# Keys and values of the second attention projected behind the routing of each group and kept in DRAM

## The reference

```
x = x + attention0(layernorm(x), ctx)          # 16 heads of 8, with biases
x = x + experts0(layernorm(x))                 # 32 experts of width 96, 4 for each token
x = x + attention1(layernorm(x), ctx, mask)    # 16 heads of 64, no biases
x = x + experts1(layernorm(x))                 # 8 experts of width 64, 2 for each token, and a shared one
# attention1
Q = (queries @ Wq) * mask;  K = (ctx @ Wk) * mask;  V = (ctx @ Wv) * mask
attn = softmax(Q K^T / 8) * mask;  attn = attn / sum(attn);  out = (attn V) @ Wo
```

## Time and profile before

| | us |
|---|---|
| median of 3 runs | 1396.31 (1390.09 to 1398.15) |
| profiled execution | 1396.49 |
| its span | 1394.7 |
| first attention | 0 to 311.5 |
| routing | 311.5 to 523.5 |
| tiles of experts | 523.5 to 663 |
| second attention, lead-in | 663 to 738 |
| second attention, steps | 738 to 1200 |
| last FFN | to 1394.7 |

### The profile page before, as it was taken

How to read it: one execution, slowest core, us unless ns; L and a number is a source line. 1 busy time by engine, 2 the same in 40 slices (tenths; PEclk the granted TensorE clock), 3 DMA queues, 4 the chain that set the end, 5 groups by cost and what they waited for, 6 DMA issues and landing times. The chain is left out here.

```text
span 1394.7 us, 27126 instructions
## 1 busy us (share of the span) xinstructions
PE 943.3 (68%) x10014; PEld 749.4 (54%) x10014; DVE 756.2 (54%) x1922; ACT 569.0 (41%) x901; POOL 604.3 (43%) x566
## 2 busy tenths in 40 slices
PE   1488778771101008998056999999999998471998
PEld 1356566540000007998024776777777778371886
DVE  3455655424554334554265676676767654267565
ACT  1166666642211104666034545544444443121554
POOL 1266775655778752444654424324241000020454
PEclk9878987755555558999579999999999999555999
DMA  4211111009111146775110000000000000100001
GB/s 131 80 58 48 55 59 53 23 8 245 40 46 42 49 144 171 202 203 159 40 40 24 20 17 24 17 18 23 17 21 6 1 2 2 34 5 0 9 23 30
DMA packets 100541, 76.33 MB, mean 55 GB/s; under 512 B 13045, under 2 KB 91810, under 8 KB 100418
## 3 DMA queue, kind: packets, MB, share of 16 engines
q1 hardware_dynamic: 61506, 43.04, 11.0%
q0 software_dynamic: 8192, 16.79, 3.9%
q10 hardware_dynamic: 30720, 14.82, 3.6%
HBM read 42.78 MB, written 31.59 MB: 53 GB/s over the span
## 5 line engine op out<-in xcount | busy, mean ns | idle before, releaser
L833 POOL DMA_INDIRECT fetched_a<-rows_y,chosen_row x128 | 122.5, 957 | 214.5 <-DVE x_all L707 178.1
L438 POOL TENSOR_TENSOR p_lo_a<-probs_a,p_hi_a 128x1024 f16<-128x1024 f32 x64 | 136.3, 2130 | 88.7 <-ACT p_hi_a L297 88.6
L588 PE MATMUL psum<-v_x_a,probs_a 128*128 128x65 f32 x1024 | 140.3, 280 | 29.8 <-DVE att_a L768 28.4
L1268 POOL DMA_INDIRECT rows_x<-rows_r,index_r x128 | 135.4, 1058 | 54.0 <-issue 39.2
L588 PEld LDWEIGHTS psum<-v_x_a,probs_a 128*128 128x128 f32 x1024 | 125.5, 193 | 46.1 <-DVE att_a L768 37.1
L752 DVE TENSOR_REDUCE negmax_a<-psum 128x8 f32<-128x1024 f32 x64 | 78.2, 1221 | 48.9 <-PE psum L571 42.9
L1423 POOL TENSOR_TENSOR h_lo_t<-hidden_t,h_hi_t 96x512 f16<-96x512 f32 x48 | 55.3, 1153 | 90.7 <-ACT h_hi_t L1395 90.7
L354 DVE TENSOR_REDUCE negmax_a<-psum 128x8 f32<-128x1024 f32 x64 | 78.3, 1223 | 26.1 <-PE psum L168 26.0
L1769 POOL TENSOR_TENSOR w_lo_f<-weighted_f,w_hi_f 128x512 fp32r<-128x512 f32 x40 | 51.9, 1297 | 93.0 <-ACT w_hi_f L1711 93.0
L296 ACT ACTIVATE probs_a<-psum 128x1024 f32<-128x1024 f32 x64 | 65.5, 1023 | 50.0 <-PE psum L152 49.8
L1054 PE MATMUL psum<-ident_x,rows_r 128*128 128x128 f16 x64 | 8.3, 310 | 114.1 <-DVE rows_r L1151 98.0
(11 more groups left out here) (336 smaller groups left out, 3137.8 us busy)
## 6 DMA issues: line engine op xcount, KB each, us to landing
listed_t<-rows_x SPq DMA_DIRECT2D x96, 128.0 KB, 2.4
rows_y<-result_t ACTq DMA_DIRECT2D x48, 256.0 KB, 2.3
q_pad_a<-narrow_q SPq DMA_DIRECT2D x64, 64.0 KB
k_x_a<-narrow_k SPq DMA_DIRECT2D x24, 128.0 KB
rows_x<-zeros_r SPq DMA_DIRECT2D x17, 128.0 KB
narrow_q<-q_hl_a SPq DMA_DIRECT2D x8, 256.0 KB, 2.0
narrow_k<-k_hl_a SPq DMA_DIRECT2D x8, 256.0 KB, 2.0
rows_x<-rows_r,index_r POOLq DMA_INDIRECT x128
```

The lines of the kernel that those rows point to most:

```text
L438: nc.gpsimd.tensor_tensor(p_lo[:, s % RING0, :], probs[:, s % NPR, :], p_hi[:, s % RING0, :], ALU.subtract).then_inc(s_plo, 1)
L588: last_ = nc.tensor.matmul(o, probs[:, s % 3, q], v_x[:, par, b % GB, h, :], start=True, stop=True)
L833: nc.gpsimd.indirect_dma_start(fetched[:, b % 2, k, :], None, rows_y, bass.IndirectOffsetOnAxis(ap=chosen["row"][:, b, k:k + 1], axis=0)). ...
L1268: nc.gpsimd.indirect_dma_start(rows_x, bass.IndirectOffsetOnAxis(ap=index[:, g * GB + t, k:k + 1], axis=0), rows[:, g % 2, t, :, :].rearra ...
```

## The change

For each group, keys and values of `attention1` are made in the routing stage. The context is masked in place by ScalarE; `keep` makes one context item, eight value items and eight key items in one run over three PSUM banks, behind ranks(g) and logits(g + 1) on TensorE, behind the scores of g + 1 on ScalarE; on VectorE their lower parts (`lower`) stand behind choose(g) and the rows of g + 1, ahead of choose(g + 1). SyncE stores them in DRAM, 2.1 MB of keys and 2.1 MB of values a group. In `attention1` SyncE loads them into the buffers that the items filled before, two groups at once and each later one when its buffer is free. The items c, k and v leave `work1`, with GpSimd's context and column. The weights are loaded and split in another order (wv and wk ahead of the first scores, w2 late, its raw copy in the place of w1's), ranks and logits share PSUM banks, and some pairs of semaphores are merged.

The core of the diff:

```diff
-    table = {0: (1, "k0 k1", ""), 1: (1, "q2 k2", "q3 k3"), 2: (1, "q4 k4", ""), 3: (1, "q5 k5", "q6 k6"),
-             4: (1, "q7 k7", ""), 5: (1, "v0 v1", "v2 v3"), 6: (1, "v4 v5", ""), 7: (1, "v6 v7", "")}
+    heads = {0: "q1", 1: "q2", 2: "q3", 3: "q4", 4: "q6", 5: "q7"}
     group = s // 8 + 1
-    head += fills(group, table[rel][1])
-    tail += fills(group, table[rel][2])
+    head += fills(group, heads.get(rel, ""))
+    if rel == 3:
+        tail += fills(group, "q5")
     if rel == 6:
         tail += fills(s // 8 + 2, "x")
     if rel == 7:
-        tail += fills(s // 8 + 2, "c q0 q1")
+        tail += fills(s // 8 + 2, "q0")
...
+        @block.sync
+        def _(sp):
+            for g in range(G):
+                if g >= 2:
+                    sp.wait_ge(s_sc, 8 * (g - 2) + 8)
+                for n in range(2):
+                    for part, k_half in enumerate((k_a, k_b)):
+                        sp.dma_start(k_half[:, g % 2, 4 * n:4 * n + 4, :], keys[g, n, :, part]).then_inc(s_keys[g % 2], 16)
+                if g >= 2:
+                    sp.wait_ge(s_pv, 2 * (8 * (g - 2) + 8))
+                for n in range(2):
+                    sp.dma_start(v_x[:, g % 2, 2 * n:2 * n + 2, :, :], vals[g, n]).then_inc(s_vals[g % 2], 16)
...
-                    await_free(("k", (b // GB, 4 * j + 3)))
+                    pe.wait_ge(s_keys[par], 64 * (b // GB // 2 + 1))
+                    await_free(("q", (b // GB, 4 * j + 3)))
...
-                        pe.wait_ge(s_vcol, s // 8 + 1)
-                        await_free(("v", (s // 8, 7)))
+                        pe.wait_ge(s_vals[par], 32 * (s // 16 + 1))
...
+        LG, RK = ([psum[:, n, 0:GB * E0], psum[:, n, 256:256 + GB * E0]] for n in (2, 3))
+        CNT, ROW = psum[:, 4, 0:128], psum[:, 4, 128:512]
+        KV = [psum[:, 5 + n, :] for n in range(3)]
...
+        parts = [(raw_later[0][:, :], w_v[0][:, :], w_v[1][:, :]), (raw_later[1][:, :], w_k[0][:, :], w_k[1][:, :]),
+                 (raw_later[2][:, :], later["wq"][0][:, :], later["wq"][1][:, :]),
+                 (raw1, record[:, :, W1_HI], record[:, :, W1_LO]),
                  (raw3[:, :, :], record[:, :, W3_HI], record[:, :, W3_LO]),
-                 (raw2[:, :, :], record[0:I0, :, W2_HI], record[0:I0, :, W2_LO])]
-        raw_later = [rt(f"raw_later{n}", [P, H * D1]) for n in range(3)]
-        parts += [(raw_later[n][:, :], later[name][0][:, :], later[name][1][:, :]) for n, name in enumerate(("wq", "wk", "wv"))]
-        raw_sel = rt("raw_sel", [P, 8, P])
+                 (raw2, record[0:I0, :, W2_HI], record[0:I0, :, W2_LO])]
+        c_hi, c_lo = rt("c_hi", [P, 512], F16), rt("c_lo", [P, 512], F16)
+        k_out, v_out = rt("k_out", [P, 2, 2, 4, 512], F16), rt("v_out", [P, 2, 2, H, D1 + 1])
+        s_masked, s_kv, s_kv_hi, s_kv_lo, s_v = (rsem(n) for n in ("masked", "kv", "kv_hi", "kv_lo", "v"))
+        s_k_out, s_v_out, s_parted = [rsem(f"k_out{n}") for n in range(2)], [rsem(f"v_out{n}") for n in range(2)], rsem("parted")
+        made = [("c", 0)] + [("v", n) for n in range(8)] + [("k", n) for n in range(8)]
+        FINE = 9
...
+                def store_values(g, n):
+                    sp.wait_ge(s_v, 8 * g + 4 * n + 4)
+                    sp.dma_start(vals[g, n], v_out[:, n, :, :, :]).then_inc(s_v_out[n], 16)
+
+                def store_keys(g, n):
+                    sp.wait_ge(s_kv_lo, FINE * g + 1 + 4 * n + 4)
+                    sp.dma_start(keys[g, n], k_out[:, n, :, :, :]).then_inc(s_k_out[n], 16)
...
+                for g in range(G):
+                    for n in range(2):
+                        store_values(g, n)
+                    for n in range(2):
+                        store_keys(g, n)
+                    if g == 3:
+                        sp.wait_ge(s_parted, 4)
+                        sp.dma_start(raw2, a["L0_ffn_w2"].rearrange("e i h -> i e h")).then_inc(s_raw[5], 16)
+                        sp.dma_start(raw_sel, a["c_sel1"]).then_inc(s_late, 16)
+                        sp.dma_start(later["wo"][:, :, :],
+                                     a["L1_xattn_Wo"].rearrange("(c p) h -> p c h", p=P)).then_inc(s_late, 16)
...
+                def keep(g, first, last):
+                    for at in range(first, last):
+                        kind, n = made[at]
+                        o = KV[(len(made) * g + at) % 3]
+                        if len(made) * g + at >= 3:
+                            older, before = divmod(len(made) * g + at - 3, len(made))
+                            if made[before][0] == "v":
+                                pe.wait_ge(s_v, 8 * older + made[before][1] + 1)
+                            else:
+                                pe.wait_ge(s_kv_lo, FINE * older + (0 if before == 0 else 1 + made[before][1]) + 1)
+                        if kind == "c":
+                            pe.wait_ge(s_masked, g + 1)
+                            for t in range(GB):
+                                last_ = nc.tensor.transpose(o[:, t * P:(t + 1) * P],
+                                                            ctx_all[:, (g * GB + t) * D:(g * GB + t + 1) * D], ident[:])
+                        elif kind == "v":
+                            if n == 0:
+                                pe.wait_ge(s_kv_lo, FINE * g + 1)
+                            if g == 0 and n == 0:
+                                pe.wait_ge(s_parted, 1)
+                            t, half_ = divmod(n, 2)
+                            cols, tok = slice(half_ * 512, half_ * 512 + 512), slice(t * P, (t + 1) * P)
+                            nc.tensor.matmul(o, c_hi[:, tok], w_v[0][:, cols], start=True, stop=False)
+                            nc.tensor.matmul(o, c_hi[:, tok], w_v[1][:, cols], start=False, stop=False)
+                            last_ = nc.tensor.matmul(o, c_lo[:, tok], w_v[0][:, cols], start=False, stop=True)
+                        else:
+                            if g == 0 and n == 0:
+                                pe.wait_ge(s_parted, 2)
+                            cols = slice(n * P, (n + 1) * P)
+                            nc.tensor.matmul(o, w_k[0][:, cols], c_hi[:, :], start=True, stop=False)
+                            nc.tensor.matmul(o, w_k[0][:, cols], c_lo[:, :], start=False, stop=False)
+                            last_ = nc.tensor.matmul(o, w_k[1][:, cols], c_hi[:, :], start=False, stop=True)
+                        last_.then_inc(s_kv, 1)
...
+                logits(0)
+                for g in range(G):
+                    ranks(g)
+                    if g + 1 < G:
+                        logits(g + 1)
+                    keep(g, 0, 17)
...
+                def masked(g):
+                    for t in range(GB):
+                        b = g * GB + t
+                        c = ctx_all[:, b * D:(b + 1) * D]
+                        last_ = nc.scalar.activation(c, c, ACT.Copy, scale=const["mask"][:, b:b + 1])
+                    last_.then_inc(s_masked, 1)
...
+                def keep(g, first, last):
+                    for at in range(first, last):
+                        kind, n = made[at]
+                        o = KV[(len(made) * g + at) % 3]
+                        act.wait_ge(s_kv, len(made) * g + at + 1)
+                        if kind == "c":
+                            nc.scalar.activation(c_hi[:, :], o, ACT.Copy).then_inc(s_kv_hi, 1)
+                        elif kind == "v":
+                            t, half_ = divmod(n, 2)
+                            b = g * GB + t
+                            if g and n % 4 == 0:
+                                act.wait_ge(s_v_out[n // 4], 16 * g)
+                            if half_ == 0:
+                                nc.scalar.activation(v_out[:, t // 2, t % 2, :, D1], const["unit"][:, :], ACT.Copy,
+                                                     scale=const["mask"][:, b:b + 1])
+                            nc.scalar.activation(v_out[:, t // 2, t % 2, half_ * 8:half_ * 8 + 8, 0:D1],
+                                                 o.rearrange("p (h d) -> p h d", d=D1), ACT.Copy,
+                                                 scale=const["mask"][:, b:b + 1]).then_inc(s_v, 1)
+                        else:
+                            if g and n % 4 == 0:
+                                act.wait_ge(s_k_out[n // 4], 16 * g)
+                            nc.scalar.activation(k_out[:, n // 4, 0, n % 4, :], o, ACT.Copy).then_inc(s_kv_hi, 1)
...
+                upper_rows(0)
+                split(0, parts[0])
+                split(1, parts[1])
+                grades(0)
+                for g in range(G):
+                    if g + 1 < G:
+                        upper_rows(g + 1)
+                        grades(g + 1)
+                    keep(g, 0, 17)
+                    if g + 1 < G:
+                        masked(g + 1)
+                    if g in (0, 1, 2):
+                        split(g + 2, parts[g + 2])
```

(42 more changed lines are left out.)

178 lines of the change are left out of this document (70 added, 108 removed).

## The result

| | median, us | of before |
|---|---|---|
| before | 1393.2 (1381.65 to 1398.15, 4 runs) | |
| after | 1492.78 (1487.09 to 1493.95, 4 runs) | 1.0715 (1.0657 to 1.0772) |

Slower, as forecast, but by 99.6 us (96.5 against the median shown ahead) where 43 were forecast. The profiled span is 1489.9 us, 95.2 more than before.

What follows compares the result with a forecast made beforehand. VectorE's in-order chain was to bound routing, as TensorE paces the second attention. Routing +104, attention running -57 and lead-in -4 gave +43 on 1396.5: 1440 us, with 1400 to 1500 for 8 in 10.

Steps and rivals of the forecast that it cites:

- terms 1 to 3: Routing: the run in VectorE's order makes groups 32.2 us, plus weight splits and last group: +91.7 us, 3 off for pads.
- term 4: Routing: VectorE's unexplained waits for ranks, 22.5 us in before, now count whole on its chain: +15 us (0 to 45).
- The third rival: Traffic stalls the supply: stores and loads lengthen unexplained waits in routing, lead-in and attention; 1498 us, chance 0.11.
- the low clock: Routing: TensorE's clock stays low, so each run takes 25.5 us, eight of them +55; 1495 us, chance 0.12.
- The likeliest: The case of VectorE's chain as worked out, bounding routing: 1440 us, own range 1405 to 1480, chance 0.67.
- The rule weighed: Instruction refills share DMA engines with queues, so 33.8 MB of stores would lengthen each refill, moving the sum nearer the third rival.
- term 5: Second attention, running: period falls to 50.3 us, gaining 8.3 in six groups and 7.3 in the last: -57 (-42 to -76).
- term 6: Second attention's lead-in: sixteen of 24 items go, against 8.5 MB of loads at the start: -4 us (-12 to +10).
- Cover holds: Rival: GpSimd's scatter, 24 us a group, stays routing's bound and the run is free; about 1348 us, chance 0.10.
- the clock never rises: Rival in routing: TensorE rests between runs, so its clock stays low and a run takes 25.5 us; 1495 us, chance 0.12.

Runs made afterwards that it cites:

- C: Chip of a later round; the changed kernel re-run there unedited: 1395.7 us, 1.0226 of before, which took 1365.11 us there.
- A: Chip of the main result, its number not recorded; changed kernel 1492.78 us against before's 1393.2 us, 1.0715.
- D: Chip of a later round; the changed kernel re-run there unedited: 1486.25 us, 1.0763 of before, which took 1379.85 us there.
- no_stores_again: Changed kernel with the routing stage's stores of keys and values left out for groups 1 to 7, on D: 1479.49 us, 1.0714 of before.
- B: Chip of the first follow-ups; before took 1367.45 us there; changed kernel with 26 dummy matmuls a group added: 1390.53 us, 1.0153 of before.
- E: Chip of a later round; the changed kernel re-run there unedited: 1392.43 us, 1.019 of before, which took 1366.16 us there.
- keys_first: Changed kernel with keys made before values and the next group's ranks amid the values on TensorE, on B: 1360.17 us, 0.995 of before.
- keys_first_2: keys_first with VectorE's weight subtraction and ScalarE's cast moved into waits: 1339.95 us, 0.982 of before on C; 1423.09 us, 1.0305 on D.

## Why the prediction was right and wrong

*The chain (terms 1 to 3) was right, and a little too long.* On C, from first scatter to pad rows, it is 241.5 us, forecast 256.0 without stalls. A clean group is 30.7 where 32.2 were forecast: the context 2.1 us (2.6), eight values 7.6 (8.1), the keys with their end 7.2 (7.5). The splits add 9 us up to the last group where 12.3 were set, and the tail after it is 17.9 (18.3). TensorE ran four items at a pitch of 0.43 and then at 0.21, as put. The stage's end was cheaper than forecast: 20.0 us from the pad rows on in place of 32.8, a gain of 12.8 for which 3 were set. The pads ran 15.1 us and not 29.5; by then the last scatters, begun at 602.15, were over, which fits but was not tested.

*The step that failed is term 4, "unexplained stalls", +15 of 0 to 45.* The same program takes 301.7 us on A and 241.5 on C for first scatter to pad rows, and before takes 166.7 and 155.2. So the stalls, with what follows from them, are 60 us of the changed kernel's routing, not 15; the chain set 14.5 too long and the end 9.8 too dear hid 24 of the 45 that are missing, and 21 show. In the clean group (36.8 and 30.7 us) 4.0 of the 6.1 lie between ScalarE's fourth and seventh eviction, 1.2 behind them, where the keys start at the lower clock, and 0.9 ahead. I had taken three waits of 22.5 us for a constant of the kernel, at a rate per time. They are a matter of the chip, and their sum in before was no measure for a kernel with other work in that place: the change put a run of 48 matmuls into every group, onto the chain, and there they come in every group.

*The third rival had the number and some of the marks, but not the cause.* It gave 1498 us; the period came over 53 in most groups, and the lead-in gained nothing, as it says. Its waits of 8 us and more did not come: ScalarE's longest is 3.6. Its cause in routing was the stores' traffic. That is refuted on D: without the stores -7 us, with twice the stores +2. That its number came near is luck, and so is that the measured 1492.8 lies within the stated 1400 to 1500: the range reached there for this rival and the low clock (whose own terms, eight times 7.3, give 1498 and not 1495), and neither is what happened. The likeliest's own range, 1405 to 1480, it leaves. The rule weighed with the rival does not explain the waits either. The Trainium skill, DMA: Bandwidth & Descriptors, section Queues, rings and completion order, lets the instruction refill share the engines with the stores; if that sharing made the waits, no_stores_again would have lost them, at a share of 0.09 in place of 0.37. How long a refill takes no run here shows. The profile's pages of A and C also list the same instruction traffic, 82 packets and 0.4% of the DMA engines' time on either.

*The attention (term 5) missed twice.* Its parts were near: the last group 42.3 (set unchanged at 43.4), the one without fetched sums 47.0 (47.3), a full one 48.7 to 50.4 on C (50.3). On A it is 51.9 to 54.9. The waits come again here: from 1000 to 1180 us TensorE's matmuls of the values (L601) wait seven times without a releaser on A, up to 1.2 us, and never on C. In the step ahead of the exponential at 990.94 there is one, and behind it the clock has fallen:

```profile
985.88 0.38 PE L618 MATMUL psum<-x_hi_a,wq_hi 128*128 128x512 f16 x1
986.09 0.38 PE L619 MATMUL psum<-x_lo_a,wq_hi 128*128 128x512 f16 x1
...
988.97 1.00 PE L601 MATMUL psum<-v_x_a,probs_a 128*128 128x65 f32 x8 [1.05 <-issue]
...
992.29 0.63 PE L618 MATMUL psum<-x_hi_a,wq_hi 128*128 128x512 f16 x1
992.71 0.63 PE L619 MATMUL psum<-x_lo_a,wq_hi 128*128 128x512 f16 x1
```

A pitch of 0.42 after 0.21 six microseconds before. In all A's full period is 4.4 us longer than C's, 22 in five groups, against the 1.9 a group that before loses to A too: 12.7 us less gain on A than on C. The other miss is a plain one: I counted seven gains between exponentials, but the first seven steps gained only 0.8 us on A and 0.5 on C. Seven lies one too high, 8 us. Why is not shown; on C the granted clock in these steps was 0.88, where it was 1.00 before, so part of the work taken out may have come back as slower matmuls. On C the whole is -44.4, forecast -57.

*The lead-in (term 6)* was +2.0 for -4, within its range.

*A reading that was off* without moving the sum: the row at 494.22 is the second scatter of group 7. The first is at 491.45, so before's groups are 23.6 us apart and not 24.0.

*The other two rivals.* *Cover holds* fell with GpSimd's idle time, and *the clock never rises* with the pitch of 0.21; holding the clock up moved a clean group by under 1 us (B) or at most 1.8 (E).

On C and E, without the waits, the change costs 30.6 and 26.3 us; on A and D, with them, 99.6 and 106.4. The forecast of +43 lies between, and is right for neither.

What makes the waits stays open. Shown is that they exist on some chips (or in what else ran there) and not on others, in every group of the run; that they depend neither on the stores nor on the weights' values; and that they cost less with a third of the matmuls. Amid the evictions on A and D the first long one of a group ends behind the rise of the clock to 2.4 GHz, also where another order puts that rise at other items. But the rise cannot be the whole cause. Before's three waits lie in a stage whose granted clock is 0.50 throughout; here is the first, with TensorE's last matmul of these ranks, and what the engines did in these us (columns as above):

```profile
337.93 0.19 PE L1075 MATMUL psum<-mark_r,half_r 128*128 128x32 f16 x1
347.07 0.29 DVE L1181 TENSOR_TENSOR placed_r<-psum,table_r 128x128 f32<-128x128 f32 x1 [7.99 <-remote]
```
```profile
340.00:350.00 10.00, 0.00 (x0) 0.00 (x0) 2.76 (x10) 0.00 (x0) 7.52 (x9) 0.50 0.49 165
```

What it has in common with the waits amid the evictions is that an engine waits for a result of TensorE whose last matmul began long before. The kernels that hold TensorE's clock up in routing ran only on chips without the waits, so they say nothing of this.

## What to carry to other kernels

Before work is put into an engine's idle time, ask whose order it enters: here TensorE and ScalarE had room for the run, but VectorE's in-order queue put all of it between two choices: on C the groups of before are 21.8 to 25.7 us apart, a clean one of the changed kernel 30.7. Put first the part that the queue's owner needs, and let the part that it doesn't need run beside its next work: the same work in that order turned 1.0226 into 0.982 on one chip, and 1.076 into 1.03 on another. And waits without a releaser in a trace are to be priced by where the change puts work, on the chain above all, and if possible by a second chip, not by their sum in the trace of before.

## What the runs showed of the hardware

- The chips fell into two kinds by before's time, 1365 to 1367 us and 1380 to 1393 us, and the changed kernel's ratio went with them: 1.02 on two of the one, 1.07 to 1.08 on two of the other. The ratio of two kernels is not a property of the kernels alone.
- On D leaving out 30 of the 34 MB of stores in routing saved 6.8 us of the whole kernel, about 1 us a group, and 67 MB cost 2.2 us more; both are within the runs' intervals.
- The packets of the first DMA queue took the same time on A and C: 22.2% of 1490 us and 23.7% of 1393 us, 330 us both. So the chips don't differ in how fast its data moved.
- A cast of 2.8 to 3.6 us and a subtraction of 3.3 to 4.4 us nearly vanished in waits of 4.3 us of the same engine once they stood in front of them: the three groups that hold them took 29.4 to 30.8 us in keys_first (on B) and 24.9 to 25.7 in keys_first_2 (on C).
- On D the same order took 31.9 to 32.0 us in groups without a subtraction ahead of the run and 26.7 to 27.9 in the three with one of 3.3 to 4.4 us: where the waits exist, a group with more work can be the shorter one.
